# Mamba window layer on one NeuronCore: softplus, normalisation and skip term moved between engines, and C broadcast by one fp32 product

## What is computed

```python
tn = (t - mu) * rsqrt(var + 1e-5) * ln_g + ln_b          # over 128 channels
xi, z = split(tn @ W_in + b_in)                          # 256 each
xc = silu(causal_conv4(xi) + conv_b)
dr, Bm, Cm = split(xc @ W_x)                             # 8, 16, 16
delta = softplus(dr @ dt_w + dt_b)                       # 256 channels
# over 64 positions, for each channel d and each of 16 states n:
h[d, n] = exp(delta[d] * A[d, n]) * h[d, n] + delta[d] * xc[d] * Bm[n]
y[d] = sum_n h[d, n] * Cm[n]
out = ((y + xc * D) * silu(z)) @ W_out + b_out + x
```

## Time and profile before

| | |
|---|---|
| median of 3 runs | 9233.19 us |
| the profiled execution | 9233.49 us |
| its span | 9231.7 us, so 1.8 us lie around it |
| PE, DVE, ACT, POOL busy | 93%, 90%, 83%, 87% of the span |
| granted TensorE clock, mean | 0.991 |
| layer 0's scans, first to last start | 105.0 to 6651.3 us |
| DMA | 931.99 MB, mean 101 GB/s |

### The profile page before, as it was taken

The page is one execution under the profiler, slowest core; times in us unless marked ns, Lnnn a source line. Parts: engine busy times, 40 slices in busy tenths (PEclk is TensorE's granted clock), DMA queues, the critical chain, the costliest instruction groups (busy, mean ns, idle before and its releaser), DMA issues. The chain is left out here.

```text
span 9231.7 us, 162156 instructions
## 1 busy us (share of the span) xinstructions
PE 8609.1 (93%) x54525; PEld 6725.1 (73%) x54525; DVE 8294.6 (90%) x8144; ACT 7704.9 (83%) x13926; POOL 8062.4 (87%) x3865
## 2 busy tenths in 40 slices
PE   7999999999999999999999999999799999999999
PEld 4666666666666666666666666666689999999788
DVE  5999999999999999999999999999889999999766
ACT  6999999999999999999999999999755555555577
POOL 5999999999999999999999999999789999999500
PEclk9999999999999999999999999999999999999999
DMA  3333333333333333333333333333311111110255
GB/s 92 109 120 111 118 110 120 113 116 111 121 113 115 112 120 115 113 113 119 117 110 114 120 115 110 114 122 113 100 39 34 37 36 34 37 37 33 90 185 181
DMA packets 648481, 931.99 MB, mean 101 GB/s; under 512 B 79960, under 2 KB 277600, under 8 KB 643552
## 3 DMA queue, kind: packets, MB, share of 16 engines
q1 hardware_dynamic: 647904, 924.64, 31.8%
HBM read 778.38 MB, written 146.04 MB: 100 GB/s over the span
## 5 line engine op out<-in xcount | busy, mean ns | idle before, releaser
L1035 POOL TENSOR_TENSOR prod<-state,c_all 128x1024 f32<-128x1024 f32 x1280 | 3028.2, 2371 | 72.6 <-DVE state L909 72.6
L1024 POOL TENSOR_TENSOR drive_d<-du,b_all 128x1024 f32<-128x1024 f32 x1024 | 2424.3, 2368 | 13.7 <-issue 12.4
L909 DVE TENSOR_TENSOR_SCAN state<-decay_d,drive_d 128x1024 f32<-128x1024 f32 x1024 | 2336.9, 2282 | 77.1 <-ACT decay_d L724 77.0
L909 DVE TENSOR_TENSOR_SCAN state<-decay_r,drive_r 128x1024 f32<-128x1024 f32 x1024 | 2323.4, 2269 | 27.9 <-PE drive_r L581 16.1
L594 PEld LDWEIGHTS y_acc<-ident,prod 128*128 128x128 f32 x16384 | 1867.2, 142 | 630.8 <-issue 524.3
L594 PE MATMUL y_acc<-ident,prod 128*128 128x128 f32 x16384 | 2160.0, 276 | 42.4 <-POOL prod L1035 38.5
L1332 DVE SCALAR_TENSOR_TENSOR sum_d<-bank_d,filt,sum_d 128x512 f32<-128x512 f32 x2470 | 1654.2, 742 | 119.2 <-PE bank_d L1240 119.2
L737 ACT ACTIVATE ub<-ut,bt 128x256 f32<-128x256 f32 x4096 | 1739.1, 500 | 12.4 <-PE drive_r L581 12.0
L1379 POOL TENSOR_TENSOR sum_p<-sum_p,scaled 128x1024 f32<-128x1024 f32 x650 | 1555.1, 2392 | 79.0 <-ACT scaled L1290 31.3
L1290 ACT ACTIVATE scaled<-bank_p,filt 128x512 f32<-128x512 f32 x1560 | 945.5, 689 | 621.6 <-PE bank_p L1240 613.3
L724 ACT ACTIVATE decay_d<-delta,neg_a 128x504 f32<-128x504 f32 x2048 | 1312.0, 674 | 79.8 <-DVE state L909 78.7
(11 more groups left out here) (155 smaller groups left out, 14646.3 us busy)
## 6 DMA issues: line engine op xcount, KB each, us to landing
c_all<-bc_rows SPq DMA_DIRECT2D x1280, 256.0 KB, 3.3
b_all<-bc_rows SPq DMA_DIRECT2D x1024, 256.0 KB, 3.8
ys<-row_spectra SPq DMA_DIRECT2D x130, 256.0 KB, 2.8
column_sums<-tt SPq DMA_DIRECT2D x130, 256.0 KB, 2.1
x_in<-in_x_dram SPq DMA_DIRECT2D x64, 512.0 KB, 4.9
x_res<-in_x_dram SPq DMA_DIRECT2D x64, 512.0 KB, 5.0
x_rows<-x SPq DMA_DIRECT2D x64, 512.0 KB, 4.5
row_spectra<-z SPq DMA_DIRECT2D x64, 512.0 KB, 3.7
```

Source lines behind the costliest of these rows:

```text
L909: dve.tensor_tensor_scan(state[n % NT][:].rearrange("p h t -> p (h t)"), decay[:].rearrange("p h w t -> p (h w t)"), drive[:].rearrange("p ...
L1024: pool.tensor_tensor(drive_d[place_of(DSTEPS, n, ND)][:], du[:, :, q * HT:(q + 1) * HT], b_all[slot][:].unsqueeze(1).to_broadcast([P, 2, HT]),
L1035: pool.tensor_tensor(prod[n % NP][:], state[n % NT][:], c_all[slot][:].unsqueeze(1).to_broadcast([P, 2, HT]), ALU.mult).then_inc(s["prod_g ...
```

## The change

The schedule tables `JOBS`, `AT`, `BY_GPSIMD` are replaced. `BY_GPSIMD` grows from 20 to 23 steps, so `BY_VECTOR` shrinks from 12 to 9. C is kept as one fp32 row per state and broadcast by one fp32 product, whose stationary operand is one column of the identity read 128 times; `take_low` goes. The bias of dt comes from an 89th row of `dt_w` against a row of ones. ACT makes |v| only, DVE makes max(v, 0) + log part in one instruction, so `add_soft` on POOL goes. The mean's product becomes a centring product (identity minus mean), its result stays in the bank until DVE multiplies it by the reciprocal root (`normalise`), so `centre` and `make_tn` go, and `tn` has its own buffer. The skip term becomes the first product of the `turn` jobs (4 long ones a block). B by token is made by transposes of 88 rows. Three of four `take_ut` go from DVE to ACT. `UB_AT` and `Z1_BY_VECTOR` are empty, so the DVE versions of `scale_u` and `make_z1` never run; the rings' slots are counted through blocks.

```diff
-BY_GPSIMD = tuple(sorted(RSTEPS + (8, 12, 18, 20)))
+BY_GPSIMD = (1, 3, 4, 5, 7, 8, 9, 11, 12, 13, 14, 15, 17, 18, 19, 21, 23, 24, 25, 26, 27, 29, 31)
 JOBS = [
-    (0, "z00", "front", 0), (0, "xp1", "scan", 1), (3, "conv00", "front", 1), (7, "z10", "front", 0),
-    (8, "turn10", "back", 0), (8, "dt01", "scan", 1), (10, "dt11", "scan", 1), (12, "bt1", "scan", 0),
-    (12, "conv10", "front", 1), (15, "turn11", "back", 0), (18, "z01", "front", 0), (18, "conv01", "front", 1),
-    (19, "ut01", "scan", 0), (22, "conv11", "front", 1), (24, "ut11", "scan", 0), (27, "z11", "front", 0),
-    (28, "out0", "back", 1), (31, "out1", "back", 1), (35, "xp0", "front", 1), (37, "turn00", "scan", 0),
-    (37, "dt00", "front", 1), (41, "dt10", "front", 1), (42, "mean0", "ahead", 0), (44, "mean1", "ahead", 0),
-    (48, "turn01", "scan", 0), (48, "var0", "ahead", 1), (49, "var1", "ahead", 1), (50, "ut00", "front", 1),
-    (51, "ut10", "front", 0), (51, "fy0", "tail", 1), (53, "bt0", "front", 0), (58, "fy1", "tail", 1),
+    (0, "z10", "front", 0), (0, "xp1", "scan", 1), (3, "z00", "front", 1), (4, "conv00", "front", 1),
+    (8, "turn10", "back", 0), (9, "dt01", "scan", 1), (11, "dt11", "scan", 0), (13, "turn11", "back", 1),
+    (15, "conv10", "front", 1), (16, "z01", "front", 0), (18, "ut01", "scan", 0), (20, "bt1", "scan", 0),
+    (20, "z11", "front", 1), (22, "conv01", "front", 1), (23, "ut11", "scan", 0), (25, "conv11", "front", 0),
+    (29, "out0", "back", 1), (31, "out1", "back", 0), (34, "xp0", "front", 1), (37, "dt10", "front", 0),
+    (38, "dt00", "front", 1), (40, "mean0", "ahead", 1), (45, "var0", "ahead", 0), (48, "ut00", "front", 0),
+    (50, "turn01", "scan", 0), (50, "mean1", "ahead", 1), (52, "var1", "ahead", 0), (55, "turn00", "scan", 0),
+    (58, "ut10", "front", 1), (60, "bt0", "front", 0), (61, "fy0", "tail", 1), (63, "fy1", "tail", 1),
 ]
+UT_BY_SCALAR = ('ut10', 'ut01', 'ut00')
 AT = {
...
-    "softplus0": 43, "softplus1": 13, "silu": 34, "take_bt": (54, 13), "square": (45, 48), "deviation": (47, 50),
-    "less_mean": 52, "deviation1": 55, "z1": (3, 5, 19, 21), "yo": (52, 59),
+    "softplus0": 39, "softplus1": 12, "silu": 33, "take_bt": (59, 21), "square": (43, 51), "deviation": (46, 55),
+    "less_mean": 58, "deviation1": 42, "z1": (9, 9, 13, 26), "yo": (62, 63),
...
-    "delta0": (43, 45), "delta1": (15, 15), "du0": (46, 48), "du1": (15, 21), "edge": 27, "shift1": 63,
-    "tn": (56, 60),
+    "tn": (47, 56), "take_dt0": (40, 41), "take_dt1": (14, 14), "take_ut0": (50, 59),
+    "du0": (41, 51), "du1": (18, 18), "edge": 29, "shift1": 63,
-    "x_in": 15, "rows": (17, 0), "rows_landed": (24, 6), "x1_out": 16, "x_res": 25, "yo_out": 26,
+    "x_in": 17, "rows": (21, 0), "rows_landed": (22, 2), "x1_out": 15, "x_res": 14, "yo_out": 28,
 }
...
-                pe.matmul(c_bank[:], wt["pick"][:, n % NS, :], c_rows[q][:], start=True,
+                pe.matmul(c_bank[:], wt["ident"][0:NS, n % NS:n % NS + 1].to_broadcast([NS, P]), c_rows[q][:], start=True,
                           stop=True).then_inc(s["c_full"], 1)
...
+                    pe.matmul(misc[:], wt["diag_d"][:, hf, :], xc[par][:, hf, q * HT:(q + 1) * HT], start=True,
+                              stop=False, skip_group_check=True)
...
-                    if n in SKIP_AT and S.scan:
-                        add_skip(p, (n - ADD_BEHIND) // NS, SKIP_AT[n])
...
-                act.activation(c_rows[q][:], misc[0:LOW + NS, :], ACT.Copy).then_inc(s["c_high_done"], 1)
+                act.activation(c_rows[q][:], misc[0:NS, :], ACT.Copy).then_inc(take(S, f"xp{q}"), 1)
...
             def softplus(S, M, q):
-                taken(act, S, f"dt0{q}", f"dt1{q}")
+                for hf in range(2):
+                    misc = full(act, S, f"dt{hf}{q}")
+                    act.activation(soft[:, hf, :], misc[:], ACT.Abs).then_inc(s["softplus_done"], 1)
...
+            def normalise(S, q):
+                misc = full(dve, S, f"mean{q}")
+                need(dve, s["rstd_done"], (S.m + 2) * 2 + q + 1)
...
+            def take_dt(S, hf, q):
+                M = S.m + 1 if q == 0 else S.m
+                misc = full(dve, S, f"dt{hf}{q}")
+                need(dve, s["softplus_done"], M * 8 + 4 * q + 4)
...
+                dve.scalar_tensor_tensor(delta[:, hf, q * HT:(q + 1) * HT], misc[:], 0.0, soft[:, hf, :], ALU.max,
+                                         ALU.add).then_inc(take(S, f"dt{hf}{q}"), 1)
...
-            def make_du(M, q, hf, p):
-                need(pool, s["delta_done"], (M * 2 + q) * 2 + hf + 1)
+            def make_du(S, M, q, hf, p):
+                taken(pool, S, f"dt{hf}{q}")
```

More of the change, by code:

```diff
@@ L111, in upto, with scaled_by, place_of @@
     return M * len(steps) + nth(steps, n + 1)
[L114 to L115 removed]
+def scaled_by(vector):
+    return tuple(n for n in RSTEPS if (n in UB_AT) == vector)
+def place_of(steps, M, n, ring):
+    return (M * len(steps) + nth(steps, n)) % ring
 def before_in(steps, M, n, ring):
[L120 to L122 removed]
+    i = M * len(steps) + nth(steps, n) - ring
+    return i // len(steps), steps[i % len(steps)]
 def nth_load(steps, M, n, ring):
[L127 to L128 removed]
+    return (M * len(steps) + nth(steps, n)) // ring + 1
 class Slot:
@@ L424, in layer0 @@
         du = sb("du", [P, 2, BT])
-        rows = sb("rows", [XR, HT])
-        c_rows = [sb(f"c_rows{q}", [LOW + NS, HT], F32R) for q in range(2)]
+        rows = sb("rows", [96, HT])
+        c_rows = [sb(f"c_rows{q}", [NS, HT]) for q in range(2)]
         bt = [sb(f"bt{q}", [P, 4, NS]) for q in range(2)]
@@ L467, in full, with filled @@
             return job_bank[S.bank[name]]
+        def filled(eng, S, *names):
+            for bank in range(2):
+                for name in [j[1] for j in S.mine if j[1] in names and j[3] == bank][-1:]:
+                    need(eng, job_full[bank], S.before[name] + 1)
         def taken(eng, S, *names):
@@ L479, in scanned, with z1_made @@
             need(eng, s["scan_done"], M * NSTEP + n + 1)
+        def z1_made(eng, m, quarters):
+            by_v = len(Z1_BY_VECTOR)
+            done = sum(i < quarters for i in Z1_BY_VECTOR)
+            need(eng, s["z1_v_done"], m * by_v + done if done else 0)
+            need(eng, s["z1_done"], m * (4 - by_v) + quarters - done if quarters > done else 0)
         def multiplied(eng, M, n):
@@ L542, in body @@
                         if S.front:
[L543 removed]
+                            full(sp, S, "z00")
                         load_x(x_in, after, s["x_ready"])
@@ L697, in body @@
                 for n in range(NSTEP):
-                    if n + 1 in RSTEPS and S.scan:
+                    if n + 1 in RSTEPS and n not in RSTEPS and S.scan:
                         turn_drive(S.step(n + 1, p))
@@ L704, in body @@
                         add_state(S.step(n - ADD_BEHIND, p))
-                    if n in SKIP_AT and S.scan:
-                        add_skip(p, (n - ADD_BEHIND) // NS, SKIP_AT[n])
                     jobs(S, p, 2 * n + 1)
+                    if n + 1 in RSTEPS and n in RSTEPS and S.scan:
+                        turn_drive(S.step(n + 1, p))
+                if S.ahead:
+                    taken(pe, S, "mean0", "mean1")
             slots(pe, body, blocks)
@@ L756, in take_front @@
                         hf, q = int(name[-2]), int(name[-1])
-                        if name == "z01" and S.back:
+                        if name in ("z01", "conv01", "conv11") and S.back:
                             taken(act, S, "turn10", "turn11")
@@ L871, in others @@
                 for i in range(4):
-                    if h == AT["z1"][i] and S.tail:
+                    if h == AT["z1"][i] and S.tail and i not in Z1_BY_VECTOR:
                         make_z1(m, i)
@@ L880, in body @@
                     others(S, p, 2 * n)
+                    if n + 1 == NS and S.scan:
+                        taken(act, S, "dt01", "dt11")
+                    if n + 1 == NSTEP and S.front:
+                        taken(act, S, "dt00", "dt10")
                     if (n + 1) % NSTEP in DSTEPS and S.step(n + 1, p):
@@ L932, in take_low @@
-            def take_low(S, M, q):
-                misc = full(dve, S, f"xp{q}")
-                need(dve, s["c_high_done"], M * 2 + q + 1)
-                dve.tensor_tensor(c_rows[q][LOW:LOW + NS, :], misc[LOW:LOW + NS, :],
-                                  c_rows[q][LOW:LOW + NS, :].bitcast(F32), ALU.subtract).then_inc(take(S, f"xp{q}"), 1)
+                need(dve, s["rstd_done"], (S.m + 2) * 2 + q + 1)
+                if S.front:
+                    filled(dve, S, "z00", "z10", "z01", "z11", "conv00", "conv10", "conv01", "conv11")
@@ new lines, in normalise, with scale_u @@
+                dve.tensor_tensor(tn[:, q * HT:(q + 1) * HT].rearrange("p (n r c) -> p r n c", n=HWN, r=WS),
+                                  misc[:].rearrange("p (r n c) -> p r n c", r=WS, n=HWN),
```

(31 more changed lines are left out.)

185 lines of the change are left out of this document (79 added, 106 removed), and 3 rows, old and new, of the table AT.

## The result

The changed kernel takes 9555.45 us (median of 4 runs, 9553.31 to 9561.0) against 9231.79 before: a ratio of 1.0352, 95% interval 1.0339 to 1.0365. Slower by 324 us, where 9080 was forecast, so 476 us lie between forecast and result. Layer 0's scans run from 116.0 to 6977.0 us (first to last start), instead of 105.0 to 6651.3: a block takes 107.2 us instead of 102.3, where 99.9 was forecast, and the pipeline's fill ahead of them takes 11 us more.

A forecast was written before the change was run, and what follows sets the result against it. No engine alone was the bound: four lay within 2 us, taking turns along a chain. Chain -3.0 plus 0.6 of new waits gave -2.4 us a block, 64 x -2.4 = -154, so 9233.5 became 9080; range 8940 to 9190.

The forecast's parts named there:

- The price of C's product: C's broadcasts on PE: 12 at 0.58 = 7.0 us a block become 9 at 0.86 = 7.7, +0.7.
- PE's sum: PE's total work a block: -0.2 us from C's broadcasts, skip and bt together, to 94.2.
- The new wait: ACT waiting at take_bt, DVE's take_dt waiting behind ACT's |v|, exp and log: 0.6 us a block charged for both.
- -2.4 on PE up to ut01, -0.6 on ACT: Chain of a block: PE's stretch up to ut01 2.4 us shorter, ACT's stretch 0.6 net, together -3.0 us.
- Steps 8 to 15: Sign: over 25 us there would mean POOL's seven products were too dense and prove the forecast wrong.
- ACT's z wait: Sign: ACT's waits for the z jobs under 1 us a block; at 3.4 the PE step failed.
- the 98% that it announced: Sign: POOL busy close to 98% of layer 0's steps, which would last near 6396 us.
- late loads of B: Rival: B's load for step 4, behind the row store, makes POOL wait up to 2.7 us; 9374 us, chance 0.12.
- the sums of POOL, ACT and DVE: Work a block after the change: POOL 96.0 us, ACT 95.5, DVE 91.5.
- softplus's wait of POOL gone: Sign: POOL's wait for softplus gone, a shorter wait of du for DVE's delta in its place.
- layer 1 unchanged: Layer 1, behind layer 0's steps, keeps its code but for small constants, so the difference comes from layer 0's 64 blocks.
- The setup, taken at 0: Setup ahead of the steps: 0 to -2 us in total, taken as 0 since everything there waits for weight loads.

The follow-up runs named there:

- b_f64: Kernel before with C broadcast by one fp32 product of 64 rows, 12 a block, all else as before: 9494.81 us, one run.
- b_f88: Kernel before with C broadcast by one fp32 product of 88 rows, 12 a block, all else as before: 9331.42 us, ratio 1.0112.
- a_dtact: Changed kernel with the softplus stage alone undone (ACT takes both parts of dt, POOL adds), C's 16-row fp32 product kept: 9365.25 us, ratio 1.0142.
- a_f88: Changed kernel with C's fp32 product over 88 rows instead of 16: 9315.56 us, ratio 1.0096 to the kernel before.
- a_c_fp32r: Changed kernel with C broadcast as before, by the 48-row fp32r product of a high and a low part: 9224.13 us, ratio 0.9991.
- a_r88: Changed kernel with C by the fp32r product of a high and a low part over 88 rows: 9194.01 us, ratio 0.9959.

## Why the prediction was wrong

- **The price of C's product** is the term that failed, of size and of place. The prediction took "the fp32 one", 0.86 us, from products of 88 to 128 rows, and set the bounds at 0.42 and 0.86 with a hidden weight load. A product of 16 rows takes 1.05 and 0.15 around it. Nine of them are 10.8 us, not 7.7. The earlier trace rows had the hint: the 0.10 ahead of and 0.06 behind the 48-row product were counted as belonging to fp32r, and left out for the new form, where they belong to the small number of rows. Of the 476 us, 331 are the form of C as a whole, of which 240 are the rows, the slower clock that goes with them included.
- **PE's sum** of 94.2 was 98.3. With 88 rows, and so with the price that the prediction used, it was 94.5: the other terms were right. The 3.8 between are 3.1 of the product, and the rest goes with the lower clock, for which the sum had no term. Up there a microsecond of PE's busy time reached the time in full (240 us, 3.75 a block, for 3.8), in the kernel before in part (b_f64 to b_f88 at the same clock: 163 us, 2.6 a block, for 3.5), and below 94 a saved one hardly (21 us, 0.3 a block, for 2.5). The sum treated both sides of the balance alike.
- **The new wait** was named, priced at 0.6 for DVE and ACT, and put at the wrong engine. The prediction listed what stands behind `take_dt` in DVE's queue, but not who waits for the bank that it empties. PE's mean0 has the same bank at the same half-step, and turn11 comes one half-step ahead of the take. That is 6 us of PE standing a block, and a slower clock behind it. What it costs in time is not shown by itself: a_dtact gained 190 us, but it also moves work between engines, and PE still stood 2.9 us for the load of x; with a light PE, moving the stand changed nothing.
- **"-2.4 on PE up to ut01, -0.6 on ACT"** came in part and did not reach the block. From the first z job to ut01, before, in the changed kernel and in a_f88:

```profile
2973.76 1.10 PE L636 MATMUL job_bank<-x_in,z_w 128*128 128x512 f32 x2
...
3022.87 1.02 PE L645 MATMUL job_bank<-tn,z_w 128*128 128x512 f32 x2
3055.79 0.60 PE L670 MATMUL job_bank<-ident,du 128*128 128x128 f32 x4
...
3016.37 1.09 PE L645 MATMUL job_bank<-tn,z_w 128*128 128x512 f32 x2
3048.29 0.60 PE L670 MATMUL job_bank<-ident,du 128*128 128x128 f32 x4
```

Before it was 33.1 us, to 3006.84; the prediction's 32.0 counted back one mean block from the next one's start, and the trace has that start at 2973.76. Then 32.9 in the changed kernel and 31.9 in a_f88, each with 2.1 of stand at the turn job inside. So at the price that the prediction used the stretch lost 1.2 of the 2.4, with the stand inside, which the prediction did not have. Behind ut01 the block got longer instead: in a_c_fp32r, with PE's sum under the forecast, the whole gave 0.9991 and not 0.983. There lie the stand at mean0 and DVE's wait of 3.2 us ahead of the scan of step 15. The row names ACT's decay, but in the block above PE's turned drive starts at 3072.10, takes 1.03, and the scan starts at 3073.22; PE came to it late, behind four convolution parts. a_c_fp32r and a_r88 wait there as long. How much each of them holds back, and whether ACT's -0.6 came, was not separated.
- **The signs.** Steps 8 to 15 took 26.7 us, over the 25 that were to prove POOL too dense; but PE is busy 26.59 of them and POOL 24.59, so the sign came from PE. ACT's z wait, forecast under 1 us a block, was 2.9, near the 3.4 that were to say that the PE step failed. By the prediction's own sum POOL would have been busy 96.0 of 99.9, 96%, and not the 98% that it announced.
- **The rivals.** The slower one, late loads of B, came true as a wait (3.2 us a block, 2.7 at most forecast) and not as a cause: removing it changed nothing. The right rival, PE as the bound through the new product, was not listed, although shows two records for an fp32 product and one for C's fp32r product.
- **Right:** the sums of POOL, ACT and DVE within 0.2 us; softplus's wait of POOL gone; layer 1 unchanged within some 5 us. The setup, taken at 0, is 11 us longer to the first scan; in its fill DVE stands 5.8 and 6.3 us ahead of its two `normalise` instructions.

## What to carry to other kernels

Price a matmul by a row of the same number of contraction rows, not only of the same type and columns; where few rows are needed, pad with zero weights (72 and 88 rows were measured, both cheap) if the data are there anyway. When a take from a shared PSUM bank is moved behind another engine's result, look for the next job in that bank: the waiting engine is PE, with all its queue. In this schedule an engine 2 us below its neighbours gave next to nothing back when it got faster, and took half to all of it when it got slower. Compare the granted clock of two runs before pricing their difference by instructions alone.

## What was not expected of the hardware

- A product of 512 fp32 columns takes 0.86 us over 72 or 88 rows and 1.05 over 16 or 64; an fp32r one 0.31 over 88 rows and 0.42 over 48, with some 0.15 more lost around the small ones. All at a granted clock of 1.00, 2.4 GHz.
- A DVE sum of two SBUF operands, 0.69 us by its median, took up to 5.4 us beside POOL's work.
- Behind a stand of 4 us PE's next product took 1.87 us instead of 0.86, at the lower clock level; behind one of 3.8 the next ran at full speed and those after it at the lower level.
- Products of the same price kept PE busy 102.3 us a block at a granted clock of 0.97 and 100.6 at 1.00.
